# Which of several waits of one instruction is written first, in thirty places of a four-layer network kernel

## The chip, the cores and the metric

The kernel runs on one core of one Trainium2 chip. The metric is the device time of the core in microseconds (us), less being better. Several executions of one kernel are compared by their median.

## The reference, cut to what matters

The network takes x, 8 sequences of 256 rows of 128 numbers, and adds eight blocks to it one after the other, each behind a layer normalisation:

```python
x = x + L0_attn(layernorm(x))   # q, k, v as spike counts, 16 heads, softmax
x = x + L0_ffn(layernorm(x))    # FP4-quantized gate * up, down
x = x + L1_attn(layernorm(x))   # four Mamba layers
x = x + L1_ffn(layernorm(x))    # ternary weights, 128 -> 512
x = x + L2_attn(layernorm(x))   # causal linear attention
x = x + L2_ffn(layernorm(x))    # 8 experts of 512, top 1
x = x + L3_attn(layernorm(x))   # long convolution as two scans, projection, norm
x = x + L3_ffn(layernorm(x))    # dense 512 plus product-key retrieval, top 8
```

The core of a Mamba layer, for each of 256 channels d and 16 states s, is a recurrence over the 256 rows t:

```python
dA = jnp.exp(dt_t[:, :, None] * A)
h = dA * h + dt_t[:, :, None] * B_t[:, None, :] * u_t[:, :, None]
y = jnp.einsum('bds,bs->bd', h, C_t)
```

## The kernel before

Everything stays in on-chip memory as X, two tiles of 128 rows for each of the 8 sequences ("chunk" c). The work is cut into stages, and stages are put on five lines: `u` (setup), `f` (front), `s` (scan), `a` and `b` (the stages outside the Mamba layers, of even and odd chunks for the most part). A stage has one generator for each engine: `pe` (TensorE, PE), `dve` (VectorE, DVE), `act` (ScalarE, ACT), `pool` (GpSimd, POOL) and `sp` (SyncE, which issues the DMAs). Each `yield` ends a turn. The order of turns on each engine is written out by hand in the strings `ORDER`, and `take_turns` plays them: so each engine has one fixed list of instructions, in which the five lines alternate, and an instruction that waits holds all that stand behind it.

Each line has a semaphore for each engine, and each operation adds one to it (`then_inc`, with the name of the operation recorded by `tick`). `e.wait_ge(semaphore, value)` puts a wait before the next instruction of that engine. `n.dve("b3")` is the value that DVE's semaphore has when the operation `b3` is done. Where several waits stand before an instruction, all must come true; the order in which they are written has no part in what is computed.

The scan job k (32 of them, 8 chunks by 4 layers) works in 8 groups g of 4 states. Its steps for a group are:

- SP spreads dt and dt*u of the front over the partitions (`R[q]`, L1001); `landed` is the wait for such a transfer. `spread` is the wait for the B and C rows that the front has sent.
- ACT makes dA = exp(dt*A) in four instructions (`a`, L1025), into one of NA = 3 buffers; it waits for the scan that used the buffer last and, for g < 4, for the transfer.
- DVE multiplies dt*u by B into `dtuB`, a tile in PSUM (`b`, L1041), both inputs coming from SBUF, and then runs the recurrence over it (the scan `s`, L1049), which reads dA from SBUF and dtuB from PSUM. There is one `dtuB`, so `b` waits for the scan before it and the scan waits for `b`.
- POOL multiplies the result in place by C, in two instructions (`c`, L1060), once the scan is done.
- PE sums over the states (`y`, L1080) and frees one of NG = 6 result buffers, for which the scan six groups later waits.

The front (job k) makes dt, u, B and C for the scan; its output projection of job k - 2 is L947. The other places are in the stages of lines `a` and `b`: L643, L646 (there the copies of L427), L659, L668, L684, L698 and L711 in the attention of layer 0, L788 in its feed-forward stage, L1325 (values of the linear attention), L1390 to L1475 in the experts' stage, L1497 to L1550 in the convolution, L1620 to L1758 in the last stage.

In the experts' stage expert x has its first matrix product in L1467 (`h`), its ReLU on ACT in L1434, its second product in L1475 (`y`, over k = 0 to 3; k = 0 and k = 3 wait for ACT), and DVE adds the chosen rows to X in L1411. In the attention of layer 0 PE makes the scores of head h into one bank (L711), ACT takes the exponential (L668, `e`), and the next head's scores wait for that where there is one bank. The masks `m0` to `m3` for them are made by DVE in L627, once in the stage. `values` (L698) multiplies by v for four heads at a time.

Of the kernel before, what the change touches and what calls it, by code (L numbers as in the profile page):

```python
# [16 lines left out]
NL = 4  # L17
# [241 lines left out]
def program(nc, ap):  # L259
    with ExitStack() as ctx:  # L260
# [330 lines left out]
        class L0Attn(Stage):  # L591
# [43 lines left out]
            def pool(self, e, n, c):  # L635
# [4 lines left out]
                yield  # L640
                e.wait_ge(loaded["l0a"], 16)
                e.wait_ge(T.act, n.act("xn1"))
                e.tensor_tensor(X2(c), X2(c), row(w("l0a", "ob")), ALU.add).then_inc(T.pool, n.tick("ob"))  # L643
                yield
                e.wait_ge(U.pool, U.at(0, "pool", T.name))
                e.wait_ge(T.dve, n.dve("u3"))  # L646
# [3 lines left out]
            def act(self, e, n, c):  # L650
# [4 lines left out]
                yield  # L655
                e.wait_ge(loaded["l0a"], 16)
                e.wait_ge(T.pe, n.pe("qk"))
# [5 lines left out]
                for h in range(16):  # L663
                    if h >= 4:
                        e.wait_ge(T.pe, n.pe(f"z{h // 4 - 1}{h % 4}"))
                    e.wait_ge(T.pe, n.pe(f"s{h}"))
                    table(e, "exp")
                    e.activation(v.Pr[h % 4], score[h % len(score)], ACT.Exp, scale=SC).then_inc(T.act, n.tick(f"e{h}"))  # L668
                    yield
                yield from divide_act(e, n, T, T.banks[1], v, "z33")  # L670

            def pe(self, e, n, c):
# [7 lines left out]
                yield  # L680
                e.wait_ge(loaded["l0a"], 16)
                e.wait_ge(T.act, n.act("xT"))
# [10 lines left out]
                def values(j):  # L693
                    e.wait_ge(T.pool, n.pool("vz3"))
                    e.wait_ge(T.act, n.act(f"e{4 * j + 3}"))
# [8 lines left out]
                for h in range(16):  # L704
                    j, g = divmod(h, 4)
                    if h >= len(score):
                        e.wait_ge(T.act, n.act(f"e{h - len(score)}"))
                    if g == 0:
                        e.wait_ge(T.dve, n.dve(f"m{j}"))
# [18 lines left out]
        class L0Ffn(Stage):  # L728
# [48 lines left out]
            def pe(self, e, n, c):  # L777
# [4 lines left out]
                yield  # L782
                e.wait_ge(U.act, U.at(0, "act", "w3"))
                e.wait_ge(T.act, n.act("xT"))
# [45 lines left out]
        class Front(Stage):  # L830
# [106 lines left out]
            def pe(self, e, n, k):  # L937
                v, b = chains[k % 2], F.bank
                if k:
                    e.wait_ge(F.act, n.act(""))  # L940
                    e.wait_ge(F.dve, n.dve(""))
                if k >= 2:
                    c, l = UNITS[k - 2]
                    e.wait_ge(F.dve, n.dve("y"))
# [43 lines left out]
        class Scan(Stage):  # L988
# [22 lines left out]
            def act(self, e, n, k):  # L1011
# [4 lines left out]
                for g in range(8):  # L1016
                    at, q, h = 8 * k + g, g % 4, g // 4
                    if at >= NA:
                        job, was = divmod(at - NA, 8)
                        e.wait_ge(S.dve, S.at(job, "dve", f"s{was}"))  # L1020
                    if h == 0:
                        e.wait_ge(*self.landed(n, q, 0))
# [6 lines left out]
            def dve(self, e, n, k):  # L1029
                e.wait_ge(*self.spread(k, "B"))  # L1030
                if k == 0:
                    e.wait_ge(U.pool, U.at(0, "pool", f"wc{NL - 1}"))
                    for T in Os:
                        e.wait_ge(T.act, T.at(0, "act", "e15"))
                for g in range(8):
                    at, q, h = 8 * k + g, g % 4, g // 4
                    if at:
                        e.wait_ge(S.dve, n.dve(f"s{g - 1}") if g else S.at(k - 1, "dve", "s7"))
                    if h == 0:
# [3 lines left out]
                    yield  # L1043
                    if at >= NG:
                        job, was = divmod(at - NG, 8)
                        e.wait_ge(S.pe, S.at(job, "pe", f"y{was}"))
                    e.wait_ge(S.act, n.act(f"a{g}"))
                    e.wait_ge(S.dve, n.dve(f"b{g}"))
# [148 lines left out]
        class L2Attn(Stage):  # L1197
# [74 lines left out]
            def pe(self, e, n, c):  # L1272
# [45 lines left out]
                def values(j):  # L1318
                    e.wait_ge(T.pool, n.pool("vz3"))
                    e.wait_ge(T.act, n.act(f"p{2 * j + 1}"))  # L1320
# [31 lines left out]
        class L2Ffn(Stage):  # L1352
# [30 lines left out]
            def dve(self, e, n, c):  # L1383
                v, T = self, self.T
                enter_dve(e, n, T, c, True)
                yield from norm_dve(e, n, T, v, X2(c))
                e.wait_ge(loaded["mo"], 16)
                e.wait_ge(loaded["const"], 16)
                e.wait_ge(T.pe, n.pe("lg"))
# [12 lines left out]
                yield  # L1402
                e.wait_ge(T.act, n.act("xn1"))
                e.wait_ge(T.pe, n.pe("b2"))
# [530 lines left out]
```

## Time and profile before

| | us |
|---|---|
| three runs | 1868.27, 1875.47, 1875.95 (median 1875.47) |
| profiled execution | 1864.92 (span 1863.1) |
| PE busy, of the span | 1486.8 (80%) |
| DVE busy | 1501.9 (81%) |
| ACT busy | 1337.4 (72%) |
| POOL busy | 1241.6 (67%) |
| scans (L1049), 256 | 584.4 |
| `b` (L1041), 256 | 360.6 |
| `c` on POOL (L1060), 512 | 825.0 |

The profile is of one execution, which took less than the three runs. Its span is the time from the first to the last instruction. "Idle before" in a row is the time for which the engine did nothing just before the instructions of that row, and the names behind it say what ended that time. A chain of waits follows the last instruction back to what released it, step by step; a name with a q behind the engine (DVEq) is a step of that engine's sequencer, which waits or branches while the engine itself stays idle, and "issue" is time in which nothing that the profile shows was waited for. The chain of this profile goes back to 1243 us.

### The profile page before, as it was taken

What the parts mean: (1) busy time and instruction counts of PE and PEld (TensorE: products, weight loads), DVE (VectorE), ACT (ScalarE), POOL (GpSimd) and SP (SyncE); (2) the same over time, 40 slices, a digit from 0 to 9 for tenths busy, and PEclk for the clock granted to TensorE, in tenths of its full rate; (3) what the DMA queues carried; (4) which work ended last, traced back from release to release, by engine and by line L of the source; (5) the groups of instructions that cost most, each with busy time, mean ns of one, the idle gap of its engine ahead of it and who ended that gap; (6) DMA issues with size and microseconds to landing.
All of it is one profiled execution on the core that took longest, in us unless ns stands there. A gap on an engine that the chain in (4) does not pass through costs nothing. (4 is left out here: it accounts for less than half of the span.)

```text
span 1863.1 us, 27727 instructions
## 1 busy us (share of the span) xinstructions
PE 1486.8 (80%) x9417; PEld 1054.3 (57%) x9417; DVE 1501.9 (81%) x2326; ACT 1337.4 (72%) x2729; POOL 1241.6 (67%) x1255
## 2 busy tenths in 40 slices
PE   5767767657899987677878998778989986789975
PEld 2443434335576665544456777556667765667854
DVE  6588899899999899868898888888889998831254
ACT  4476756666898787776678878778888886654564
POOL 4158568777787778776666666777878887830046
PEclk9667677778999999677799999888999997889998
DMA  5033313423443542221235435241445432212300
GB/s 193 1 77 87 95 41 80 103 69 97 120 131 103 150 114 74 71 69 31 71 115 135 126 115 143 52 122 47 120 133 137 137 103 64 72 35 82 114 18 6
DMA packets 84588, 170.12 MB, mean 91 GB/s; under 512 B 9441, under 2 KB 14945, under 8 KB 84065
## 3 DMA queue, kind: packets, MB, share of 16 engines
q1 hardware_dynamic: 84448, 168.37, 33.1%
q8 instruction: 75, 1.23, 0.3%
q14 instruction: 65, 0.52, 0.1%
HBM read 99.12 MB, written 2.10 MB: 54 GB/s over the span
## 5 line engine op out<-in xcount | busy, mean ns | idle before, releaser
L1060 POOL TENSOR_TENSOR m<-m 128x512 f32<-128x512 f32 x512 | 825.0, 1633 | 131.0 <-DVE m L1049 125.6
L1049 DVE TENSOR_TENSOR_SCAN m<-m,dtuB 128x1024 f32<-128x1024 f32 x256 | 584.4, 2283 | 23.6 <-ACT m L1025 6.3
L1025 ACT ACTIVATE m<-m,Aneg 128x255 f32<-128x255 f32 x1024 | 428.5, 497 | 22.7 <-DMA m<-m 16.9
L1041 DVE TENSOR_TENSOR dtuB<-m 128x1024 f32<-128x1024 f32 x256 | 360.6, 1409 | 10.7 <-DMA m<-m 3.3
L1467 PE MATMUL ps<-o 128*128 128x256 f32 x512 | 149.2, 399 | 21.1 <-DVE X L1411 11.3
L1080 PE MATMUL ps<-m,w_const 128*32 128x256 f32 x2048 | 153.1, 425 | 9.6 <-POOL m L1060 9.5
L1434 ACT ACTIVATE o<-ps,w_mo 128x256 f32<-128x256 f32 x256 | 114.3, 471 | 62.1 <-PE ps L1467 60.9
L364 POOL TENSOR_TENSOR o<-o,mhalf 128x2 f32<-128x2 f32 x64 | 15.9, 249 | 202.5 <-DVE o L358 202.5
L964 PE MATMUL ps<-m,wc 128*128 128x256 f32 x512 | 138.6, 431 | 6.4 <-ACT m L385 6.4
L1475 PE MATMUL ps<-o 128*128 128x128 f32 x1024 | 129.5, 280 | 8.2 <-ACT o L1434 8.2
L1182 PE MATMUL ps<-o 128*128 128x256 f32 x512 | 123.8, 388 | 14.9 <-ACT o L1151 7.8
L1758 PE MATMUL ps<-w_const,o 128*128 128x128 f32 x512 | 89.8, 340 | 56.8 <-DVE o L1626 30.2
L1475 PEld LDWEIGHTS ps<-o 128*128 128x128 f32 x1024 | 122.5, 194 | 18.8 <-issue 13.7
L964 PEld LDWEIGHTS ps<-m,wc 128*128 128x128 f32 x512 | 110.2, 220 | 30.3 <-ACT m L385 9.3
L1758 PEld LDWEIGHTS ps<-w_const,o 128*128 128x128 f32 x512 | 82.5, 247 | 67.5 <-ACT o L1698 37.6
L668 ACT ACTIVATE o<-ps 128x512 f32<-128x512 f32 x112 | 66.2, 594 | 75.5 <-PE ps L711 48.9
L711 PE MATMUL ps<-o 32*128 32x256 bf16 x224 | 56.2, 343 | 78.9 <-ACT o L668 58.6
L1467 PEld LDWEIGHTS ps<-o 128*128 128x128 f32 x512 | 84.0, 189 | 55.1 <-ACT o L1434 22.1
L1182 PEld LDWEIGHTS ps<-o 128*128 128x128 f32 x512 | 94.2, 192 | 35.3 <-issue 15.6
L1080 PEld LDWEIGHTS ps<-m,w_const 128*32 128x32 f32 x2048 | 69.4, 120 | 77.9 <-issue 30.4
L347 ACT ACT_TABLE_LOAD x83 | 106.5, 1283 | 9.5 <-DMA w_mb<-in_mb 5.4
L1660 POOL TENSOR_TENSOR o<-o 128x512 f32<-128x512 f32 x64 | 85.9, 1343 | 15.2 <-DVE o L1620 13.6
(252 smaller groups left out, 2915.1 us busy)
## 6 DMA issues: line engine op xcount, KB each, us to landing
m<-m SPq DMA_DIRECT2D x256, 256.0 KB, 4.9
m<-spread SPq DMA_DIRECT2D x64, 512.0 KB, 4.9
o<-in_mox SPq DMA_DIRECT2D x128, 256.0 KB, 3.0
o<-in_l1x SPq DMA_DIRECT2D x88, 256.0 KB, 3.0
w_mb<-in_mb SPq DMA_DIRECT2D x1, 2288.0 KB, 12.2
m<-in_cwr SPq DMA_DIRECT2D x1, 2048.0 KB, 15.9
w_l3f<-in_l3f SPq DMA_DIRECT2D x1, 1536.0 KB, 17.4
X<-in_x SPq DMA_DIRECT2D x4, 256.0 KB, 7.1
```

Of the source, the lines that this page charges most:

```text
L347: e.preload_act_table_set("natural_log_exp_and_others")
L964: op = e.matmul(b[:, h * CH:h * CH + CH], wc[:, l, j, h * 128:h * 128 + 128], v.xT[:, j:j + CH], start=j == 0, stop=j == 3)
L1025: op = e.activation(dA[at % NA][:, j, 1:CH], R[q][:, h * CH + 1:h * CH + CH], ACT.Exp, scale=Aneg[:, l, 4 * g + j:4 * g + j + 1])
L1041: e.tensor_tensor(dtuB[:, :, :], bc(R[q][:, (2 + h) * CH:(3 + h) * CH].unsqueeze(1), 4, CH), Br[k % 2], ALU.mult).then_inc(S.dve, n.tick(f ...
L1049: e.tensor_tensor_scan(flat(G[at % NG]), flat(dA[at % NA]), flat(dtuB[:, :, :]), 0.0, ALU.mult, ALU.add).then_inc(S.dve, n.tick(f"s{g}"))
L1060: op = e.tensor_tensor(part, part, Cr[k % 2][:, j:j + 2, :], ALU.mult)
L1080: op = e.matmul(S.y[32 * q:32 * q + 32, h * CH:h * CH + CH], red, G[(8 * k + g) % NG][:, j, :], start=False, stop=j == 3, skip_group_check ...
L1182: op = e.matmul(b[:, 0:CH], v.ring[(at + j) % RING][:, cut(k)], src[:, k, :], start=k == 0, stop=k == 3)
L1434: e.activation(v.hd[x % 2][:, k, :], self.bank(5 * x + 4 + k)[:, 0:CH], ACT.Relu, bias=w("mo", "b1")[:, x, k:k + 1]).then_inc(T.act, n.tic ...
L1467: e.matmul(self.bank(5 * x + 4 + k)[:, 0:CH], v.ring[2 * x % RING][:, cut(k)], v.xT, start=True, stop=True).then_inc(T.pe, n.tick(f"h{x}{k}"))
L1475: op = e.matmul(self.bank(5 * x + 8)[:, cut(i)], v.hd[x % 2][:, k, cut(i)], v.ring[(2 * x + 1) % RING][:, cut(k)], start=k == 0 and i == 0 ...
L1758: op = e.matmul(a[:, cut(k)], v.Em[h % 2][:, cut(k)], ident, start=h == 0 and k == 0, stop=h == 3, skip_group_check=True)
```

## The change

In thirty places the order of the waits before one instruction is altered. Where a wait stood above a loop, it is now inside it under a condition, so that it still stands before the same instruction. No operation is added, taken away or moved on its engine, and no semaphore or value is another. The core of the diff:

```diff
@@ L0Attn, act (L668)
                 for h in range(16):
+                    e.wait_ge(T.pe, n.pe(f"s{h}"))
                     if h >= 4:
                         e.wait_ge(T.pe, n.pe(f"z{h // 4 - 1}{h % 4}"))
-                    e.wait_ge(T.pe, n.pe(f"s{h}"))
@@ L0Attn, pe (L711)
+                    if g == 0:
+                        e.wait_ge(T.dve, n.dve(f"m{j}"))
                     if h >= len(score):
                         e.wait_ge(T.act, n.act(f"e{h - len(score)}"))
-                    if g == 0:
-                        e.wait_ge(T.dve, n.dve(f"m{j}"))
@@ Front, pe (L947)
+                if k >= 2:
+                    e.wait_ge(F.dve, n.dve("y"))
                 if k:
                     e.wait_ge(F.act, n.act(""))
                     e.wait_ge(F.dve, n.dve(""))
                 if k >= 2:
                     c, l = UNITS[k - 2]
-                    e.wait_ge(F.dve, n.dve("y"))
@@ Scan, act (L1025)
+                    if h == 0:
+                        e.wait_ge(*self.landed(n, q, 0))
                     if at >= NA:
                         job, was = divmod(at - NA, 8)
                         e.wait_ge(S.dve, S.at(job, "dve", f"s{was}"))
-                    if h == 0:
-                        e.wait_ge(*self.landed(n, q, 0))
@@ Scan, dve (L1041 and L1049)
-                e.wait_ge(*self.spread(k, "B"))
-                if k == 0:
-                    e.wait_ge(U.pool, U.at(0, "pool", f"wc{NL - 1}"))
-                    for T in Os:
-                        e.wait_ge(T.act, T.at(0, "act", "e15"))
                 for g in range(8):
                     at, q, h = 8 * k + g, g % 4, g // 4
                     if at:
                         e.wait_ge(S.dve, n.dve(f"s{g - 1}") if g else S.at(k - 1, "dve", "s7"))
+                    if g == 0:
+                        e.wait_ge(*self.spread(k, "B"))
+                    if at == 0:
+                        e.wait_ge(U.pool, U.at(0, "pool", f"wc{NL - 1}"))
+                        for T in Os:
+                            e.wait_ge(T.act, T.at(0, "act", "e15"))
                     if h == 0:
                         e.wait_ge(*self.landed(n, q, 1))
                     e.tensor_tensor(dtuB[:, :, :], bc(R[q][:, (2 + h) * CH:(3 + h) * CH].unsqueeze(1), 4, CH), Br[k % 2], ALU.mult).then_inc(
                         S.dve, n.tick(f"b{g}"))
                     yield
+                    e.wait_ge(S.dve, n.dve(f"b{g}"))
+                    e.wait_ge(S.act, n.act(f"a{g}"))
                     if at >= NG:
                         job, was = divmod(at - NG, 8)
                         e.wait_ge(S.pe, S.at(job, "pe", f"y{was}"))
-                    e.wait_ge(S.act, n.act(f"a{g}"))
-                    e.wait_ge(S.dve, n.dve(f"b{g}"))
@@ Scan, pool (L1060)
-                e.wait_ge(*self.spread(k, "C"))
                 for g in range(8):
                     at = 8 * k + g
                     e.wait_ge(S.dve, n.dve(f"s{g}"))
+                    if g == 0:
+                        e.wait_ge(*self.spread(k, "C"))
@@ L2Ffn, dve (L1411)
                 for x in range(8):
+                    e.wait_ge(T.pe, n.pe(f"y{x}"))
                     e.wait_ge(T.dve, n.dve(f"x{x - 1}1" if x else "b2"))
-                    e.wait_ge(T.pe, n.pe(f"y{x}"))
@@ L2Ffn, act (L1434)
+                        e.wait_ge(T.pe, n.pe(f"h{x}{k}"))
                         if k == 0 and x >= 2:
                             e.wait_ge(T.pe, n.pe(f"y{x - 2}"))
-                        e.wait_ge(T.pe, n.pe(f"h{x}{k}"))
@@ L2Ffn, pe (L1475)
-                    e.wait_ge(*self.landed(n, 2 * x + 1))
                     for k in range(4):
                         if k in (0, 3):
                             e.wait_ge(T.act, n.act(f"h{x}{max(k, 2)}"))
+                        if k == 0:
+                            e.wait_ge(*self.landed(n, 2 * x + 1))
@@ L3Attn, dve (L1500)
+                e.wait_ge(T.dve, n.dve("xa"))
                 e.wait_ge(U.pool, U.at(0, "pool", "onesF"))
-                e.wait_ge(T.dve, n.dve("xa"))
@@ L3Ffn, dve (L1620)
-                    e.wait_ge(T.pe, n.pe(f"D{i}"))
                     for h in range(4):
-                        e.wait_ge(T.pool, n.pool(f"E{i}{h}"))
+                        if h % 2 == 0:
+                            e.wait_ge(T.pool, n.pool(f"E{i}{h}"))
                         if i or h:
                             e.wait_ge(T.pool, n.pool(f"w{i}{h - 1}" if h else f"w{i - 1}3"))
+                        if h % 2:
+                            e.wait_ge(T.pool, n.pool(f"E{i}{h}"))
+                        if h == 0:
+                            e.wait_ge(T.pe, n.pe(f"D{i}"))
@@ L3Ffn, pool (L1649)
+                            e.wait_ge(T.pool, n.pool(f"r{i}"))
                             e.wait_ge(T.dve, n.dve(f"fl{i}"))
-                            e.wait_ge(T.pool, n.pool(f"r{i}"))
```

The other places exchange two or three waits in the same way: at L643, L659, L684, L1390, L1497, L1524, L1550 and L1721 a value of another engine (`xn1`, `qk`, `xT`, `lg`, `gl`) now stands before the load of a weight pack; at L646 `u3` before a setup value; at L698 and L1325 ACT's `e` or `p` before POOL's `vz3`; at L788 `xT` before `w3`; at L1405 `b2` before `xn1`; at L1509 `o` before `pb`; at L1758 for h = 0 ACT's `w{i}0` before DVE's `x` or `d`.

## Rows read from the trace of the kernel before

**Rows 1.** Page, part 1: busy us, share of the span and instructions of each engine.

```profile
PE 1486.8 (80%) x9417; PEld 1054.3 (57%) x9417; DVE 1501.9 (81%) x2326; ACT 1337.4 (72%) x2729; POOL 1241.6 (67%) x1255
```

**Rows 2.** Busy time by stretch: us; PE, PEld, DVE, ACT, POOL; granted clock; DMA.

```profile
300.00:1640.00 1340.00, 1094.86 (x7100) 795.26 (x7098) 1181.14 (x1688) 1039.70 (x2130) 1007.24 (x961) 0.90 0.37 99
1650.00:1750.00 100.00, 97.39 (x652) 77.87 (x653) 18.62 (x76) 46.37 (x100) 6.17 (x24) 0.97 0.26 82
```

**Rows 3.** Chain of waits, 1420 to 1436 us: start us, us, what.

```profile
1425.92 0.03 issue
1425.95 0.05 DVEq L1048
1426.00 0.04 issue
1426.04 2.30 DVE m L1049
1428.34 0.03 DVEq L1040
...
1428.42 2.36 DVE dtuB L1041
...
1433.20 0.02 issue
1433.22 1.23 DVE dtuB L1041
```

**Rows 4.** DVE by line: count, busy us, mean ns, idle before and releasers.

```profile
L1049 DVE TENSOR_TENSOR_SCAN m<-m,dtuB 128x1024 f32<-128x1024 f32 x256 | 584.4, 2283 | 23.6 <-ACT m L1025 6.3 <-PE ps L1080 1.8
L1041 DVE TENSOR_TENSOR dtuB<-m 128x1024 f32<-128x1024 f32 x256 | 360.6, 1409 | 10.7 <-DMA m<-m 3.3
```

**Rows 5.** Timeline of DVE and POOL at 284 us: start us, us, what.

```profile
284.23 2.35 DVE L1041 TENSOR_TENSOR dtuB<-m 128x1024 f32<-128x1024 f32 x1
...
284.21 3.48 POOL L1060 TENSOR_TENSOR m<-m 128x512 f32<-128x512 f32 x2 [0.16 <-DVE m L1049]
```

**Rows 6.** Timeline of DVE and POOL around 425 us, a steady stretch.

```profile
425.39 1.23 DVE L1041 TENSOR_TENSOR dtuB<-m 128x1024 f32<-128x1024 f32 x1
...
429.08 1.23 DVE L1041 TENSOR_TENSOR dtuB<-m 128x1024 f32<-128x1024 f32 x1
...
421.76 3.53 POOL L1060 TENSOR_TENSOR m<-m 128x512 f32<-128x512 f32 x2 [0.16 <-DVE m L1049]
```

**Rows 7.** Chain of waits before L1475 (k = 3, then k = 0), L1060 and L1649.

```profile
1388.43 0.04 issue
1388.47 0.71 PE ps L1475 x4
...
1520.63 0.14 issue
1520.76 1.41 PE ps L1475 x5
...
1565.45 0.07 issue
...
1820.91 0.02 issue
1820.93 0.02 POOLq L1647
1820.95 0.09 issue
```

**Rows 8.** Who waited for whom: us in total, times, longest us.

```profile
PEld ps L711 <- ACT o L668: 92.0, 75, 4.3
```

**Rows 9.** Timeline of DVE and POOL at 764 us; chain at 1560 us.

```profile
763.34 4.82 POOL L1060 TENSOR_TENSOR m<-m 128x512 f32<-128x512 f32 x3
...
764.57 1.23 DVE L1041 TENSOR_TENSOR dtuB<-m 128x1024 f32<-128x1024 f32 x1
...
1560.64 2.39 DVE dtuB L1041
```

More of the change, by code:

```diff
@@ L640, in pool @@
                 yield
+                e.wait_ge(T.act, n.act("xn1"))
                 e.wait_ge(loaded["l0a"], 16)
-                e.wait_ge(T.act, n.act("xn1"))
                 e.tensor_tensor(X2(c), X2(c), row(w("l0a", "ob")), ALU.add).then_inc(T.pool, n.tick("ob"))
                 yield
+                e.wait_ge(T.dve, n.dve("u3"))
                 e.wait_ge(U.pool, U.at(0, "pool", T.name))
-                e.wait_ge(T.dve, n.dve("u3"))
                 spread_pool(e, n, T, v.va)
@@ L655, in act @@
                 yield
+                e.wait_ge(T.pe, n.pe("qk"))
                 e.wait_ge(loaded["l0a"], 16)
-                e.wait_ge(T.pe, n.pe("qk"))
                 for i, name in enumerate(("q", "k")):
@@ L680, in pe @@
                 yield
+                e.wait_ge(T.act, n.act("xT"))
                 e.wait_ge(loaded["l0a"], 16)
-                e.wait_ge(T.act, n.act("xT"))
                 for i, name in enumerate(("q", "k")):
@@ L693, in values @@
                 def values(j):
+                    e.wait_ge(T.act, n.act(f"e{4 * j + 3}"))
                     e.wait_ge(T.pool, n.pool("vz3"))
-                    e.wait_ge(T.act, n.act(f"e{4 * j + 3}"))
                     for kt in range(2):
@@ L782, in pe @@
                 yield
+                e.wait_ge(T.act, n.act("xT"))
                 e.wait_ge(U.act, U.at(0, "act", "w3"))
-                e.wait_ge(T.act, n.act("xT"))
                 for i in range(2):
@@ L1318, in values @@
                 def values(j):
+                    e.wait_ge(T.act, n.act(f"p{2 * j + 1}"))
                     e.wait_ge(T.pool, n.pool("vz3"))
-                    e.wait_ge(T.act, n.act(f"p{2 * j + 1}"))
                     for i in range(2):
@@ L1386, in dve @@
                 yield from norm_dve(e, n, T, v, X2(c))
+                e.wait_ge(T.pe, n.pe("lg"))
                 e.wait_ge(loaded["mo"], 16)
                 e.wait_ge(loaded["const"], 16)
-                e.wait_ge(T.pe, n.pe("lg"))
                 e.tensor_tensor(v.lg, self.bank(1)[:, 0:16].rearrange("p (a b) -> p a b", a=2), bc(w("mo", "gb").unsqueeze(1), 2, 8),
@@ L1402, in dve @@
                 yield
+                e.wait_ge(T.pe, n.pe("b2"))
                 e.wait_ge(T.act, n.act("xn1"))
-                e.wait_ge(T.pe, n.pe("b2"))
                 e.tensor_tensor(X2(c), ps2(self.bank(3)), X2(c), ALU.add).then_inc(T.dve, n.tick("b2"))
@@ L1493, in dve @@
                 yield from norm_dve(e, n, T, v, X2(c))
+                e.wait_ge(T.act, n.act("xT"))
                 e.wait_ge(loaded["l3a"], 16)
                 e.wait_ge(U.dve, U.at(0, "dve", "r7"))
-                e.wait_ge(T.act, n.act("xT"))
                 e.tensor_tensor(v.xa, v.xT, Apow[:, :], ALU.mult).then_inc(T.dve, n.tick("xa"))
+                e.wait_ge(T.dve, n.dve("xa"))
                 e.wait_ge(U.pool, U.at(0, "pool", "onesF"))
-                e.wait_ge(T.dve, n.dve("xa"))
                 e.tensor_tensor_scan(v.sc, bc(onesF[:, 0:1], CH), v.xa, 0.0, ALU.mult, ALU.add).then_inc(T.dve, n.tick("s0"))
@@ L1506, in dve @@
                 yield
+                e.wait_ge(T.pe, n.pe("o"))
                 e.wait_ge(T.pool, n.pool("pb"))
-                e.wait_ge(T.pe, n.pe("o"))
                 e.tensor_tensor(v.r, ps2(T.banks[1]), v.xn, ALU.add).then_inc(T.dve, n.tick("r"))
@@ L1521, in pool @@
                 yield
+                e.wait_ge(T.act, n.act("xT"))
                 e.wait_ge(loaded["l3a"], 16)
-                e.wait_ge(T.act, n.act("xT"))
                 e.tensor_tensor(v.xn, v.xn, row(w("l3a", "pb")), ALU.add).then_inc(T.pool, n.tick("pb"))
@@ L1546, in pe @@
                 yield
+                e.wait_ge(T.act, n.act("gl"))
                 e.wait_ge(loaded["l3a"], 16)
-                e.wait_ge(T.act, n.act("gl"))
                 for i in range(2):
@@ L1716, in pe @@
                 yield
+                e.wait_ge(T.act, n.act("xT"))
                 e.wait_ge(loaded["l3f"], 16)
-                e.wait_ge(T.act, n.act("xT"))
                 for k in range(2):
@@ L1751, in pe @@
                         yield
-                    e.wait_ge(T.dve, n.dve(f"x{i - 1}" if i else "d"))
                     for h in range(4):
                         e.wait_ge(T.act, n.act(f"w{i}{h}"))
+                        if h == 0:
+                            e.wait_ge(T.dve, n.dve(f"x{i - 1}" if i else "d"))
                         if h == 2:
```

## The prediction

> **What bounds the kernel now.** I read the page first: PE is busy 80% of the span, DVE 81%, ACT and POOL about 70% [rows 1]. No engine is full, so the stages matter. Between 300 and 1640 us, where the scans run, DVE is busy 1181 of 1340 us (88%); from 1650 to 1750 us PE is busy 97.39 of 100 us and DVE 18.62 [rows 2]. Each engine runs a fixed list in order, so a late instruction holds all behind it. The chain of waits for the scans then shows what one hand-over costs, and that is all this change can alter [rows 3].
>
> In it a scan (L1049) that comes straight after its `b` (L1041) begins 0.03 + 0.05 + 0.04 = 0.12 us after `b` ends, and the middle piece is DVEq L1048, a step of DVE's sequencer. The next `b` begins 0.02 us after that scan. The scan writes three waits (`y`, `a`, `b`), the `b` at 1433.22 one. PE shows the same: L1475 with two waits (k = 0) starts 0.14 us after ACT, with its single wait (k = 3) 0.04 us after [rows 7]. POOL's L1649 has such a step too (POOLq L1647). I conclude: the wait written first rides on the instruction, which is already queued when it comes true; the others sit in a separate step ahead, and if the last to come true is there, the engine still has to pass the step and fetch the instruction. The Trainium skill, "Perfetto Trace Analysis", Identifying Dependency Chains, says that extra waits may go into inserted EventSemaphore instructions; the trace agrees, with 0.05 us for DVEq L1048.
>
> **The change part by part.** No operation moves and no semaphore step disappears; only which wait rides changes.
>
> *Scan after `b` (L1046 to L1048).* In the timeline 118 of 256 scans follow their `b` directly (first at 118.86 us, last at 1613.40). The idle time before L1049 fits: 118 x 0.13 = 15.3, plus 6.3 for ACT and 1.8 for PE, is 23.4 of the 23.6 us shown [rows 4]. With `b` riding, each 0.12 should become 0.02: 118 x 0.10 = 11.8 us on DVE. In the other scans another DVE instruction stands between and hides the step: nothing. Where `a` is late (8 times) it stays in the step: nothing. Where `y` is last (3 idle times) 0.06 is lost each.
>
> *First `b` of a job (L1028 to L1041, g = 0).* Today `spread` rides and the previous scan stands in the step. The chain shows the result: the step at 1428.34, `b` at 1428.42, 0.08 after the scan, and it takes 2.36 us instead of 1.23 [rows 3]. Why: the multiply of POOL (L1060) waits for the same scan with its own riding wait and is a hair earlier; the first such pair starts at 284.21 (POOL) and 284.23 (`b`, 2.35 us) [rows 5]. A `b` that starts ahead of POOL takes 1.23. So 1.13 us is the price of losing that race. By the timeline 15 of the 32 first `b`s lose it so. After the change `b` starts 0.02 us after the scan and POOL 0.07 after it [rows 7], so `b` wins: 15 x (1.13 + 0.06) = 17.8 us on DVE. POOL's pair then lasts some 0.05 longer, as in the steady pairs, 3.53 against 3.48 [rows 5, 6]; nobody near the end waits for that. The Trainium skill, "SBUF — State Buffer", Who interferes with whom, says that a DVE instruction with two SBUF inputs contends with a GpSimd one that reads SBUF, and that issue order decides who blocks. That agrees with `b` (both inputs in SBUF) and with the scan, which reads one from PSUM and stays at 2.29.
>
> *All other places.* What a late wait costs in a step with one wait, against riding: POOL 0.02 + 0.02 + 0.09 = 0.13 before L1649 against 0.07 before L1060, so 0.06; PE 0.14 against 0.04, so 0.10 at most [rows 7]. For DVE I take 0.07, between POOL's 0.06 and the 0.10 of a step with two waits. No row shows ACT; from 0 to 0.10 are its ends, and I take 0.06 for it and for PE, since POOL's row is the one that shows the step itself. By the timeline the late wait sits in the step, with the engine idle for it, about 60 times on DVE (L1411 27, L1620 about 15 net, L1500 8, the rest L1390, L1405, L1509), 86 on ACT (L668 41, L1434 26, L1025 13, L659 6), 88 on PE (L1475 27, L947 17, the others 2 to 9 each) and 50 on POOL (L1060 21, L1649 16, L427 7, the rest 3 each). Sum: 4.2 + 5.2 + 5.3 + 3.0 = 17.7 us over four engines. Losses: at L711 the mask `m{j}` is made long before `e{h-1}` is there for h = 4, 8, 12, so this edit is the wrong way round. PE's weight loads wait there for ACT's L668 92.0 us in all [rows 8]; 13 of the 24 such waits come with an idle PE: 0.8 us. At L668 `z` is last 15 times: 0.9 us. Moving a DMA's wait (L1041, L1475, L1025) moves no DMA: SP's list is untouched, and a transfer that is late holds the same instruction as before.
>
> *What of it lies on the path.* The chain of waits covers the last 617 us. It holds 13 DVEq L1048 pieces, two of the five lost races of that stretch, and 22 other late waits in a step. 13 x 0.10 + 2 x 1.19 + 22 x 0.065 = 5.1 us in 617. Scaled by what the whole run has (118 against 23 direct hand-overs, 15 against 5 races, three times 22 others): 6.7 + 7.1 + 4.3 = 18 us. Paths beside it get shorter too, but not by as much everywhere, and cap the gain; I take 16 us. Bounds: if DVE were the path throughout, 11.8 + 17.8 + 4 = 34 us; if only the short gaps count and half of them, 6 us.
>
> **The rivals.** *POOL takes the port in the steady pairs (slower).* This is the place where the gain can turn. In the stretch at 425 us a scan and a `b` repeat every 3.69 us, and POOL needs 3.53 of them: its pair from 421.76 ends at 425.29, `b` starts at 425.39 [rows 6]. With 0.10 us less per period POOL ends as `b` starts. If `b` then found the port taken by POOL's next instruction it would take 2.36. Against it: a `b` at 764.57 started while POOL was in a run of three without a pause (763.34 to 768.16) and took 1.23 [rows 9], so starting in the tail of a POOL instruction can cost nothing; and POOL's next pair can't start before 0.07 after the scan, when `b` has begun. For it: the `b` at 1560.64 took 2.39 although POOL's instruction was about to end [rows 9]. It costs 1.13 a time; of 126 such pairs 16 lost eat the 18 us, and about a quarter (31, those whose POOL pair ends latest) would give 31 x 1.13 - 18 = 17 us more, times a path share of two thirds: about 1887 us.
>
> *The race is not won.* If `b` still comes second, the 7.1 us stay away: 11 us less a tenth, 1866 us.
>
> *Hidden elsewhere.* L1411 waits in DVE's list for PE, and from 1650 us PE is full [rows 2]; the freed time is waited away there: about 4 us, 1871 us.
>
> *It does nothing.* The lifecycle of a DVE instruction in the Trainium skill, "Perfetto Trace Analysis", Per-engine timelines, draws one wait queue in which all semaphores are satisfied; by that alone the order of writing would cost nothing. As a mechanism here: step and instruction pass at once whichever wait is last; 1875 us. The 0.12 against 0.02 in [rows 3] speak against it.
>
> **How the numbers follow.** The profiled execution took 1864.9 us (span 1863.1), below the three runs (1868.3 to 1876.0, median 1875.5); a change in stalls shifts both alike, so 1863.1 becomes 1847 and the median 1875.5 - 16 = 1859.5 us. Chances: forecast 0.70, race not won 0.12, hidden 0.08, nothing 0.04, slower 0.06. The range takes in the 34 us (1841) and reaches up to the case of nothing, 1875. About 0.5% (9.4 us) is what a measurement of this kernel can tell from no change. Faster by more than that: 0.70 and half of the second case, 0.76; within it: the other half, hidden and nothing, 0.18; slower 0.06.
>
> **What would show it.** In the profile after: idle before L1049 down from 23.6 to about 12 us; mean of L1041 down from 1409 to about 1340 ns, with `b` at 1.23 after a job's last scan; the step DVEq L1048 ahead of the end of `b`, so gone from the chain; L1649 and L1475 (k = 0) released in 0.07 and 0.04 us; L711 after L668 slower by 0.06 at h = 4, 8, 12. Wrong if L1041's mean rises (the port), or if these gaps shrink and the span doesn't.

## The result

| | before | after |
|---|---|---|
| runs, median (us) | 1875.47, 5 runs (1868.27 to 1876.88) | 1857.8, 5 runs (1854.7 to 1863.42) |
| ratio, with 95% interval | | 0.9922 (0.9894 to 0.9951) |
| profiled execution (us) | 1864.92, clock 0.878 | 1863.42, clock 0.864 |

A second measurement, on another occasion, gave 1871.01 us before (18 runs) and 1857.36 after (9 runs), a ratio of 0.9937 (0.9912 to 0.9963). The change makes the kernel 0.6 to 0.8% faster, 12 to 15 us. The ratios are those of the record and not quotients of the medians, which are 0.9906 (17.7 us) and 0.9927; both lie inside the intervals. The forecast was 1859.5 us.

The two profiled executions differ by 1.5 us only: that of before was faster than all five of its runs, and that of after was the slowest of its five. So the totals of these two traces say little, and what follows is read from their parts.

The profile after, page, part 1 (busy us, share of the span, instructions), to be held against [rows 1]:

```profile
PE 1502.0 (81%) x9417; PEld 1067.4 (57%) x9417; DVE 1492.5 (80%) x2326; ACT 1336.9 (72%) x2729; POOL 1240.3 (67%) x1255
```

DVE has 9.4 us less work with the same 2326 instructions. PE has 15.2 us more with the same 9417. Its granted clock fits that: a mean of 0.878 before and 0.864 after, with the two levels 2.4 and 1.2 GHz, is by estimate (1 - 0.878)/0.5 x 1863.1 = 455 us at the lower level before and 506 us after. Most of this isn't the work of the change: nine runs of the changed kernel ran between 0.863 and 0.878 (mean 0.870), and the 18 runs of the kernel before beside them between 0.866 and 0.882 (mean 0.873). The two traces also differ already in the first 100 us, before the first scan. Busy time by stretch (PE, PEld, DVE, ACT, POOL; granted clock; DMA), before and then after:

```profile
0.00:100.00 100.00, 65.38 (x330) 33.74 (x331) 63.94 (x159) 51.40 (x99) 29.28 (x70) 0.79 0.28 101
```

```profile
0.00:100.00 100.00, 66.12 (x326) 33.84 (x327) 64.08 (x159) 50.95 (x98) 27.35 (x69) 0.71 0.27 98
300.00:1640.00 1340.00, 1106.78 (x7110) 807.55 (x7109) 1176.39 (x1691) 1040.06 (x2131) 1009.29 (x962) 0.89 0.37 99
1650.00:1750.00 100.00, 97.65 (x654) 78.45 (x654) 18.24 (x74) 45.59 (x97) 6.17 (x24) 0.97 0.25 80
```

The last two lines answer [rows 2]: the stages are bound as before, DVE 88% busy between 300 and 1640 us and PE 98% from 1650 to 1750 us.

DVE by line after (count, busy us, mean ns, idle before and releasers). The scan is now L1051 and `b` is L1043; this answers [rows 4]:

```profile
L1051 DVE TENSOR_TENSOR_SCAN m<-m,dtuB 128x1024 f32<-128x1024 f32 x256 | 584.5, 2283 | 16.5 <-ACT m L1026 5.4 <-issue 3.6 <-PE ps L1083 2.8
L1043 DVE TENSOR_TENSOR dtuB<-m 128x1024 f32<-128x1024 f32 x256 | 349.7, 1366 | 9.5 <-DMA m<-m 3.1
```

The steps themselves are as many as before: in both traces the sequencers pass 651 semaphore steps on DVE, 385 on ACT, 543 on PE and 89 on POOL. So nothing was gained by having fewer of them; what changed is which wait sits in them.

The idle time before the scan is down from 23.6 to 16.5 us, and `b` takes 1366 instead of 1409 ns, 10.9 us in all. The chain of waits after (start us, us, what) shows the hand-overs of [rows 3] in the new form:

```profile
1560.85 0.02 issue
1560.87 2.30 DVE m L1051
1563.17 0.02 issue
1563.19 1.23 DVE dtuB L1043
```

and in two other places, the second product of an expert with k = 0 (0.04 where [rows 7] had 0.14) and POOL's L1657 (0.07 where it had 0.02 + 0.02 + 0.09):

```profile
1518.57 0.04 issue
1518.61 3.78 PE ps L1479 x16
...
1820.93 0.07 issue
1821.00 0.63 POOL o L1657
```

### The profile page after: what moved, and what is told of

The parts are those of the page before. It is cut to its first block, busy times and chain, and to the rows that moved or that the text cites. A ratio compares the mean times of both kernels' runs of the same rounds, so it can differ in the third digit from the quotient of the medians.

```text
span 1861.6 us, 27727 instructions
## 1 busy us (share of the span) xinstructions
PE 1502.0 (81%) x9417; PEld 1067.4 (57%) x9417; DVE 1492.5 (80%) x2326; ACT 1336.9 (72%) x2729; POOL 1240.3 (67%) x1255
## 3 DMA queue, kind: packets, MB, share of 16 engines
q8 instruction: 75, 1.23, 0.3%
## 4 chain that ended last, share of the span: by engine, by line
PE 48%; ACT 19%; DVE 18%; POOL 8%; issue 5%; DMA 2%; SPq 0%; DVEq 0%; ACTq 0%; POOLq 0%
DVE m L1051 6%; PE ps L1083 5%; ACT m L1026 4%; PE ps L1470 4%; POOL m L1063 4%; PE ps L965 4%; PE ps L1317 4%; PE ps L1185 4%; PE ps L1479 3%; DVE dtuB L1043 3%; PE ps L1767 3%; PE ps L1328 2%; PE ps L698 2%; PE ps L711 2%; ACT o L668 2%
## 5 line engine op out<-in xcount | busy, mean ns | idle before, releaser
L1051 DVE TENSOR_TENSOR_SCAN m<-m,dtuB 128x1024 f32<-128x1024 f32 x256 | 584.5, 2283 | 16.5 <-ACT m L1026 5.4
L1026 ACT ACTIVATE m<-m,Aneg 128x255 f32<-128x255 f32 x1024 | 428.5, 497 | 19.6 <-DMA m<-m 14.4
L1043 DVE TENSOR_TENSOR dtuB<-m 128x1024 f32<-128x1024 f32 x256 | 349.7, 1366 | 9.5 <-DMA m<-m 3.1
L1479 PE MATMUL ps<-o 128*128 128x128 f32 x1024 | 130.4, 281 | 7.6 <-ACT o L1437 6.8
L1185 PE MATMUL ps<-o 128*128 128x256 f32 x512 | 125.2, 391 | 12.5 <-ACT o L1154 6.7
L1479 PEld LDWEIGHTS ps<-o 128*128 128x128 f32 x1024 | 124.3, 196 | 17.7 <-ACT o L1437 13.5
L1767 PE MATMUL ps<-w_const,o 128*128 128x128 f32 x512 | 91.4, 344 | 53.1 <-DVE o L1634 31.6
L668 ACT ACTIVATE o<-ps 128x512 f32<-128x512 f32 x112 | 66.2, 594 | 76.9 <-PE ps L711 48.4
L1767 PEld LDWEIGHTS ps<-w_const,o 128*128 128x128 f32 x512 | 84.6, 252 | 63.4 <-ACT o L1706 54.8
L711 PE MATMUL ps<-o 32*128 32x256 bf16 x224 | 57.0, 348 | 78.0 <-ACT o L668 59.0
L1185 PEld LDWEIGHTS ps<-o 128*128 128x128 f32 x512 | 94.9, 193 | 32.9 <-issue 15.3
```

The lines of the kernel that those rows point to most:

```text
L1026: op = e.activation(dA[at % NA][:, j, 1:CH], R[q][:, h * CH + 1:h * CH + CH], ACT.Exp, scale=Aneg[:, l, 4 * g + j:4 * g + j + 1])
L1043: e.tensor_tensor(dtuB[:, :, :], bc(R[q][:, (2 + h) * CH:(3 + h) * CH].unsqueeze(1), 4, CH), Br[k % 2], ALU.mult).then_inc(S.dve, n.tick(f ...
L1051: e.tensor_tensor_scan(flat(G[at % NG]), flat(dA[at % NA]), flat(dtuB[:, :, :]), 0.0, ALU.mult, ALU.add).then_inc(S.dve, n.tick(f"s{g}"))
L1185: op = e.matmul(b[:, 0:CH], v.ring[(at + j) % RING][:, cut(k)], src[:, k, :], start=k == 0, stop=k == 3)
L1479: op = e.matmul(self.bank(5 * x + 8)[:, cut(i)], v.hd[x % 2][:, k, cut(i)], v.ring[(2 * x + 1) % RING][:, cut(k)], start=k == 0 and i == 0 ...
L1767: op = e.matmul(a[:, cut(k)], v.Em[h % 2][:, cut(k)], ident, start=h == 0 and k == 0, stop=h == 3, skip_group_check=True)
```

## The experiments

All ratios are to runs of the kernel before on the same chip, measured beside the others: 1870.78 us (35 runs) for the three parts and the later POOL alone; 1871.01 (18 runs) for the whole change again, its wrong places and the four steps more; 1870.47 (27 runs) for the two steps more, the parts taken out and the later POOL on top of the change. Their intervals are about 0.2% (4 us) to each side, so that single parts of this change can only just be told from nothing.

### The change in three parts

Before, with the waits of the scan alone written as in the change:

```diff
+                    e.wait_ge(S.dve, n.dve(f"b{g}"))
+                    e.wait_ge(S.act, n.act(f"a{g}"))
                     if at >= NG:
                         job, was = divmod(at - NG, 8)
                         e.wait_ge(S.pe, S.at(job, "pe", f"y{was}"))
-                    e.wait_ge(S.act, n.act(f"a{g}"))
-                    e.wait_ge(S.dve, n.dve(f"b{g}"))
```

> The kernel before with one edit alone: before the scan (L1049) the wait for `b` is written first. My theory: the 118 scans that follow their `b` directly start 0.035 us after it instead of 0.13; idle time before L1049 falls by about 11 us, b's durations stay as they are (mean 1409 ns, some 15 first `b`s of a job at 2.35 us), and the time falls by the path share of 11.4 us, 5 to 7 us (ratio 0.997). Rival (POOL takes the port in the steady pairs): L1041's mean rises and the time does not fall. Rival (order of writing does nothing): idle before L1049 stays 23.6 us and the time stays.

Before, with the first `b` of a job alone:

```diff
-                e.wait_ge(*self.spread(k, "B"))
...
                 for g in range(8):
...
+                    if g == 0:
+                        e.wait_ge(*self.spread(k, "B"))
```

> The kernel before with one edit alone: before the first `b` of a job the wait for the previous scan is written first, `spread` and the transfer after it. My theory (a race for the port): the 15 first `b`s that took 2.35 us take 1.23, the mean of L1041 falls from 1409 to about 1345 ns, idle before L1049 stays at 23.6 us; the time falls by 5 to 7 us (ratio 0.997). Rival (only the short gap counts): `b` still takes 2.35 us and the time falls by less than 1 us.

The change without these two places:

> The changed kernel with the two edits of DVE's part of the scan (L1041 and L1049 of before) undone; all other places stay changed. My theory: the first `b`s still lose the race, idle before the scan stays at 23 to 24 us, the late waits of POOL, PE and ACT are released 0.06 us earlier; the time falls by about 4 us (ratio 0.998), so most of the gain is not here. Rival (the gain is spread over all places by their number): 28 of 30 places are here, so most of the 14 us would be.

| kernel | median (us) | ratio (95%) | scan behind `b`, gap (ns) | idle before the scan (us) | mean of `b` (ns) | first `b`s over 2 us |
|---|---|---|---|---|---|---|
| before | 1870.78 | | 132 | 23.6 | 1409 | 16 |
| scan alone | 1863.41 | 0.9960 (0.9938 to 0.9982) | 35 | 14.4 | 1415 | 15 |
| first `b` alone | 1862.39 | 0.9952 (0.9933 to 0.9970) | 133 | 26.9 | 1341 | 2 |
| the rest alone | 1867.01 | 0.9984 (0.9961 to 1.0008) | 132 | 25.5 | 1405 | 16 |
| whole change | 1857.8 | 0.9922 (0.9894 to 0.9951) | 35 | 16.5 | 1366 | 4 |

(The gap is the median over the 125 scans whose `b` is the DVE instruction just before them; the whole change was measured on another occasion, beside runs of the kernel before at 1875.47 us.) Each part moves its own quantity; the idle time moves by some 3 us by itself. With the scan alone the times of `b` stay as they were:

```profile
L1049 DVE TENSOR_TENSOR_SCAN m<-m,dtuB 128x1024 f32<-128x1024 f32 x256 | 584.5, 2283 | 14.4 <-ACT m L1025 4.8 <-PE ps L1080 4.3 <-issue 0.7
L1041 DVE TENSOR_TENSOR dtuB<-m 128x1024 f32<-128x1024 f32 x256 | 362.2, 1415 | 12.9 <-DMA m<-m 5.8
```

In us, at 1871: 7.5 for the scan, 9.0 for the first `b`, 3.0 for the rest. The last one's interval includes no change at all, so that part is not shown.

### The race for the port, without touching DVE

Before, with one satisfied wait more, and so a step, ahead of POOL's product behind the eighth scan. It makes POOL later there and takes nothing away:

```diff
                     at = 8 * k + g
+                    if g == 7:
+                        e.wait_ge(U.pool, U.at(0, "pool", "onesF"))
                     e.wait_ge(S.dve, n.dve(f"s{g}"))
```

> The kernel before, and nothing is made earlier: POOL's multiply of the last group of each job (g = 7) gets a second wait, long true, which is written first, so that its wait for the scan stands in a step and POOL starts about 0.065 us later. My theory of the race: POOL at 0.13 us after the scan now comes behind the first `b` of the next job at 0.08, so the slow first `b`s fall from 15 to nearly 0 and the kernel gets faster by 5 to 7 us although one instruction is only delayed. Rival (the gain at the first `b` is that of its wait alone): nothing gets faster, the time is the same or up to 1 us more.

It came out at 1863.86 us, 0.9969 (0.9946 to 0.9992): delaying an engine made the kernel faster. Three first `b`s took over 2 us, `b` went from 1409 to 1349 ns on average, while the idle time before the scan did not fall:

```profile
L1049 DVE TENSOR_TENSOR_SCAN m<-m,dtuB 128x1024 f32<-128x1024 f32 x256 | 584.6, 2284 | 27.4 <-ACT m L1025 10.8 <-PE ps L1082 1.2
L1041 DVE TENSOR_TENSOR dtuB<-m 128x1024 f32<-128x1024 f32 x256 | 345.3, 1349 | 11.4 <-DMA m<-m 4.4
```

In these jobs `b` still starts 91 ns after the scan, as before, but POOL now starts 53 ns behind it instead of 12 ns ahead. The same edit on top of the change, where `b` is first anyway:

> The changed kernel, with one satisfied step more ahead of POOL's product behind the eighth scan, the edit that alone made the kernel before 0.31% faster. Theory (that edit helped only since it let DVE's first b take the port first, which the changed kernel does anyway): no gain, within 0.15% of the changed kernel, ratio to the kernel before 0.992 to 0.995, first b's over 2 us stay at 4 or fewer. Rival (a later POOL helps in another way, by what it does to the rest of DVE's or PE's work): 0.2% or more faster again, a ratio under 0.991.

1858.93 us, 0.9944 (0.9922 to 0.9967), three first `b`s over 2 us: no gain over the change's 0.9922 and 0.9937, and the rival's ratio under 0.991 lies outside the interval. As far as 0.2% can be told, a later POOL helps by the race and not otherwise.

### The whole change again, and its wrong places

The same kernel as the change, measured once more:

> The changed kernel as it is, to stand beside the two that follow on the same chip. Ratio to before 0.992 as first measured (0.9894 to 0.9951).

1857.36 us, 0.9937 (0.9912 to 0.9963); gap 35 ns, two first `b`s over 2 us, 19.3 us idle before the scan. So that idle time, 16.5 and 19.3 us in two executions of one kernel, is itself uncertain by some 3 us; over all seven traces here in which the scan's waits stand in the new order it is 13.4 to 19.3 us.

The change with L711 and L668 (h = 4, 8, 12) written the other way:

```diff
+                    if h >= 4 and h % 4 == 0:
+                        e.wait_ge(T.pe, n.pe(f"z{h // 4 - 1}{h % 4}"))
                     e.wait_ge(T.pe, n.pe(f"s{h}"))
-                    if h >= 4:
+                    if h >= 4 and h % 4:
                         e.wait_ge(T.pe, n.pe(f"z{h // 4 - 1}{h % 4}"))
...
-                    if g == 0:
-                        e.wait_ge(T.dve, n.dve(f"m{j}"))
                     if h >= len(score):
                         e.wait_ge(T.act, n.act(f"e{h - len(score)}"))
+                    if g == 0:
+                        e.wait_ge(T.dve, n.dve(f"m{j}"))
```

> The changed kernel with its two wrong-way places mended: at L711 ACT's `e` is written first again, at L668 `z` for h = 4, 8, 12 and `s` else. My theory: 12 idle waits of PE (0.104 to 0.042 us) and 15 of ACT (0.083 to 0.024) shrink, 1.6 us in sum, of which about a third to a half lies on the path: 0.5 to 1 us less than the changed kernel, too little for the clock to tell; the waits in the trace tell it. Rival (the attention of layer 0 sets the pace of the first 400 us): the full 1.6 us.

1859.63 us, 0.9926 (0.9898 to 0.9953). With the same done in four more places where the trace showed the late wait in the step (L1122, L1147, L1185, L1767):

> As the one before, and four further places: PE's L1767 (h = 2) writes `a5` first, DVE's first product and ACT's SiLU of the layer-1 feed-forward write the partner first, PE's second products there write ACT's wait before that for the transfer. My theory: some 10 waits of PE, 8 of ACT, 5 of PE and 3 of DVE shrink by 0.06: 1.6 us in sum, below 1 us on the path; in all 1 to 2 us faster than the changed kernel (ratio to before about 0.991). Rival: no difference or slower, since a transfer is last in some of them.

1856.79 us, 0.9920 (0.9894 to 0.9947). Both are the same as the change within the interval; a term of 2 us can't be measured here. No version that beats the change by a measurable amount came out of this.

### More steps

Before, with eight satisfied waits more at each scan, four ahead of `b` and `a` in the text and four behind. They make four steps more, and all four come to stand behind the step that waits for `b`:

```diff
+                    for _ in range(2):
+                        e.wait_ge(U.pool, U.at(0, "pool", "onesF"))
+                        e.wait_ge(U.act, U.at(0, "act", "A"))
                     e.wait_ge(S.dve, n.dve(f"b{g}"))
                     e.wait_ge(S.act, n.act(f"a{g}"))
+                    for _ in range(2):
+                        e.wait_ge(U.pool, U.at(0, "pool", "onesF"))
+                        e.wait_ge(U.act, U.at(0, "act", "A"))
```

> The kernel before with four more sequencer steps between the one that holds `b` and the scan: eight waits, all long true, are added before each scan. My theory: each costs 0.05 us, so a scan right behind its `b` starts about 0.33 us after it instead of 0.13, 24 us more idle time on DVE, of which the path share of 0.45 to 0.57 shows: 11 to 14 us slower (ratio 1.006 to 1.008). The slope gives that share without the port, since the first `b`s are not touched. Rival (DVE sets the pace throughout): the full 24 us, 1.013. Rival (such steps are passed ahead and cost nothing): idle before the scan stays at 24 us and the time stays.

It took 1913.31 us, 1.0224 (1.0196 to 1.0251): 42 us more, above what either theory had put down. The chain of waits shows why:

```profile
1447.43 1.24 DVE dtuB L1041
1448.68 0.04 DVEq L1051
1448.71 0.05 issue
1448.76 0.05 DVEq L1053
1448.81 0.05 issue
1448.86 0.05 DVEq L1054
1448.91 0.05 issue
1448.96 0.05 DVEq L1053
1449.01 0.05 issue
1449.05 0.05 DVEq L1054
1449.10 0.04 issue
1449.15 2.30 DVE m L1055
```

A step is not only its own 0.05 us; with the issue behind it each costs 0.1 here, and the median gap of the 125 direct scans is 480 instead of 132 ns, 87 ns for each step on average. And the cover that I had counted on elsewhere is too short for them: the scans that have another DVE instruction between `b` and them, which lost nothing before, account for 18 of the added 61 us:

```profile
L1055 DVE TENSOR_TENSOR_SCAN m<-m,dtuB 128x1024 f32<-128x1024 f32 x256 | 585.0, 2285 | 84.7 <-DVE dtuB L1041 40.3 <-issue 22.1 <-ACT m L1025 17.4
```

Half of it, with one such pair of waits on each side:

> The kernel before, with two more satisfied steps behind b ahead of each of the 256 scans (half of what the kernel with four more steps carries). With four, the 125 scans directly behind b start 480 ns after it instead of 132, that is 87 ns for each step, DVE's idle time before the scan rises from 23.6 to 84.7 us, and the kernel becomes 42 us longer, 0.69 us for each us of that idle time. Theory (each step costs the same, and some 0.7 of DVE's added idle time before the scan reaches the end): a gap of 306 ns, 50 to 54 us idle before the scan, 1889 to 1894 us where the kernel before takes 1871, a ratio of 1.010 to 1.012. Rival (the first steps vanish in slack and only many are paid): a ratio under 1.006.

1884.83 us, 1.0089 (1.0067 to 1.0111), a gap of 285 ns where 306 were expected. So the first two steps added 76 ns each, and the next two, from 285 to 480 ns, 98 each:

```profile
L1053 DVE TENSOR_TENSOR_SCAN m<-m,dtuB 128x1024 f32<-128x1024 f32 x256 | 584.5, 2283 | 50.1 <-DVE dtuB L1041 27.4 <-ACT m L1025 10.4 <-issue 4.6
```

The idle time is as expected, the time a little below the 1889 to 1894 us put down. This gives the share of DVE's waiting before a scan that reaches the end: 14.4 of 26.6 us, or 0.54, for two steps (16.6 us and 0.63 by the ratio 1.0089); 42.3 of 61.1, or 0.69, for four; and with the step made harmless 7.4 of 9.2, or 0.8, where the interval of 4 us on the time also allows 0.4. It is neither nothing nor everything, and no threshold is seen from which it sets in.

### Each part taken out of the whole

The change with the first `b`'s waits as before, and the change with the scan's waits as before:

> The changed kernel with the waits of the 32 first b's written as before; all else as changed. The race for the port is lost again: 15 or 16 first b's over 2 us, mean of b 1405 to 1415 ns instead of 1366, gap from b to scan 35 ns. Alone this part brought 0.48%, the scan's order 0.40% and the rest 0.16%, together 1.04%, where the whole change brings 0.78 and 0.63% in its two measurements. Theory (the parts lie partly on the same waiting time, so each is worth less beside the others): 0.20 to 0.35% slower than the whole change, a ratio to the kernel before of 0.9955 to 0.9965. Rival (the parts simply add up and the rest is scatter): 0.45% or more slower than the whole change, a ratio of 0.998 or above.

> The changed kernel with the waits of the scan written as before; all else as changed. Gap from b to scan 132 ns, 24 to 27 us idle before the scan, mean of b 1345 to 1370, at most 4 first b's over 2 us. Theory (the parts share their gain): 0.15 to 0.35% slower than the whole change, a ratio to the kernel before of 0.995 to 0.9965. Rival (they add up): 0.40% or more slower, a ratio of 0.997 or above.

The first took 1860.42 us, 0.9944 (0.9925 to 0.9963), with 15 first `b`s over 2 us, mean 1416 ns, gap 35 ns. The second took 1863.14 us, 0.9973 (0.9953 to 0.9992), with three over 2 us, mean 1352 ns, gap 132 ns. Against 0.993 for the whole, the mean of its two ratios, the first `b` is worth 0.14% there and the scan's order 0.43%. Alone they were worth 0.48 and 0.40%. By quotients of the medians it is 0.29 and 0.44%. For the scan's order that is the rival's side. For the first `b` it is below what even the theory of shared gain had put down (0.20 to 0.35%) by the one reckoning and inside it by the other. Two intervals of 0.2% stand behind each difference, and I can't call either settled; that the first `b` still saves time beside the rest is not shown. What the runs do settle is that each of the two moves its own quantity, the gap or the time of `b`, in both surroundings.

## Why the prediction was right, point by point

**The riding wait.** It was: the first written rides, the others cost a step. Right; it explains the gaps, and with the race below the first `b`s. Scans behind `b` start 35 ns after it instead of 132, that is 97 ns less, where 100 were put down. Over the other places the time from the last semaphore to the start, with the wait in a single step and then riding, is:

| engine | in a step (ns) | riding (ns) | taken in the prediction (us saved) |
|---|---|---|---|
| DVE | 92 | 24 | 0.07 |
| ACT | 83 | 24 | 0.06 |
| POOL | 133 | 68 | 0.06 |
| PE | 105 | 42 | 0.06 |

These are medians of the waits for which the engine sat idle. The bounds 0 and 0.10 for ACT, of which no row spoke, held. Where the late wait shares DVE's step with another, it costs 120 to 123 ns. The rival "it does nothing" falls with it. One reading in the prediction was wrong and did no harm: the `b` at 1433.22 of [rows 3] has two waits and not one. The wait for its transfer stands in a step (1430.94 to 1430.96) that was passed while the scan ran, and the wait for the scan rides, so it shows the riding wait even better. The Trainium skill, "Perfetto Trace Analysis", Per-engine timelines, draws one wait queue in which all semaphores are satisfied; 35 against 132 ns shows that this holds only for the wait that rides.

**The idle time before the scan.** Forecast about 12 us, measured 16.5, 19.3 and (scan alone) 14.4. The removed term is right to 0.4 us: 118 x 0.097 = 11.4 us where 11.8 were forecast. What is left was undersized: the 118 hand-overs of the forecast keep 0.035 and not 0.02 us each, 4.1 instead of 2.4 us, and single waits of 0.2 to 3.1 us for ACT, an issue and PE make up 5.4, 3.6 and 2.8 us, where the forecast had counted the former 6.3 and 1.8 for ACT and PE.

**The first `b`.** The mechanism is right, the count of races too high. Before, 15 first `b`s started right behind the scan with POOL's product just ahead, 14 of them by 11 or 12 ns, and took 2.3 us. After, 12 of the 15 start 35 ns behind the scan, POOL follows 45 ns later, and they take 1.23. The timeline of the job of [rows 5], DVE and then POOL:

```profile
282.66 2.29 DVE L1051 TENSOR_TENSOR_SCAN m<-m,dtuB 128x1024 f32<-128x1024 f32 x1
284.98 1.23 DVE L1043 TENSOR_TENSOR dtuB<-m 128x1024 f32<-128x1024 f32 x1
286.25 2.29 DVE L1051 TENSOR_TENSOR_SCAN m<-m,dtuB 128x1024 f32<-128x1024 f32 x1
...
285.03 3.53 POOL L1063 TENSOR_TENSOR m<-m 128x512 f32<-128x512 f32 x2
```

POOL loses nothing by it, because one product of its pair is long either way: 1.27 and then 2.25 us when POOL leads (before), 2.30 and then 1.27 us when `b` leads (after).

Three are still lost, at 147.66, 978.91 and 1465.73 us:

```profile
976.54 2.29 DVE L1051 TENSOR_TENSOR_SCAN m<-m,dtuB 128x1024 f32<-128x1024 f32 x1
978.91 2.34 DVE L1043 TENSOR_TENSOR dtuB<-m 128x1024 f32<-128x1024 f32 x1
...
978.90 3.47 POOL L1063 TENSOR_TENSOR m<-m 128x512 f32<-128x512 f32 x2
```

There the wait for the spread dt*u, which stands in the step, came true only 121 to 123 ns before `b` started, about when the scan ended; passing the step then took longer than POOL took. The prediction says that moving a DMA's wait moves no DMA and holds the same instruction as before; in these three its place decides the race. In the trace of the repeated run none of the three is lost. The first `b`s' time above 1.23 us fell from 18.1 to 5.7 us, 12.4, where 15 x 1.13 = 17 was forecast. The time that the other `b`s lose to the port stayed (27.3 and 28.8 us). The mean of `b` came to 1366 and not to the forecast's 1409 - 66 = 1343 ns, 5.9 us in all: 4.6 of them are first `b`s, mostly the three lost races, and 1.4 the other `b`s. That the port is what is lost, and not something else that comes with the order, is shown by the kernel with the later POOL: 91 ns after the scan as before, and yet 1.23 us. The Trainium skill, "SBUF — State Buffer", Who interferes with whom, says that issue order decides who blocks; 12 ns of it decide over 1.1 us here.

The traces show more than a fixed price. A `b` that starts inside a product of L1060 with more than 0.15 us of it left lasts until 1.08 to 1.10 us after that product's end, in all 52 such cases of the trace before and all 42 of the trace after: before, with 0.31, 0.60, 0.82 and 1.13 us of the product left it took 1.40, 1.69, 1.91 and 2.22 us (at 1523.77, 1000.68, 1481.84 and 1147.52 us). So the 1.13 us is the price of meeting a product at its start.

**POOL in the steady pairs (the slower rival).** It did not occur. The period of scan and `b` shrank from 3.69 to 3.59 us, and POOL works through without a pause, but `b` stays at 1.23:

```profile
418.31 1.23 DVE L1043 TENSOR_TENSOR dtuB<-m 128x1024 f32<-128x1024 f32 x1
419.58 2.29 DVE L1051 TENSOR_TENSOR_SCAN m<-m,dtuB 128x1024 f32<-128x1024 f32 x1
421.90 1.23 DVE L1043 TENSOR_TENSOR dtuB<-m 128x1024 f32<-128x1024 f32 x1
...
414.77 13.08 POOL L1063 TENSOR_TENSOR m<-m 128x512 f32<-128x512 f32 x7 [0.28 <-DVE m L1051]
```

POOL's next product can't start before the scan is done, and by then `b` is ahead of it by 45 ns. The tail of POOL's former pair costs `b` nothing: with 1 to 18 ns of a product left ten `b`s of this trace took 1.22 to 1.23 us, and six with 106 to 139 ns left as well. The `b` at 1560.64 of [rows 9], which the rival rested on, had 58 ns of a product left, but POOL's next product began 17 ns behind it and took 1.27 us, while `b` took 2.38: the tail was not what cost it.

**The losses.** As forecast in place and size: at L711 ACT's wait is in the step, 104 against 43 ns, 12 times with an idle PE; at L668 `z` is last exactly at h = 4, 8 and 12, 83 against 23 ns, 15 times. Together 0.7 + 0.9 us of engine time. That they cost the kernel anything was not measurable.

**What reaches the end.** The forecast was 6.7 us for the scan, 7.1 for the race and 4.3 for the rest, 18 in all, with 16 taken. Measured alone: 7.5, 9.0 and 3.0 us, each to within 4 us. The whole: 14.6 and 11.8 us. The share of the scan's term was taken as 6.7/11.8 = 0.57; the runs with more steps give 0.54 (0.63 by the ratio) and 0.69. That the terms come out so near is in part luck, two errors that cancel. Less time went from DVE than forecast: 9.2 us of idle time before the scan for 11.8, and 15.3 us of the first `b`s' time for 17 (12.4 in the whole change). And a larger share of it reached the end, by the medians and ratios some 0.8 for the scan and 0.6 for the race alone, where 0.57 and 0.40 were taken; the later POOL, with much the same saved on `b`, gives 0.4, so this share is known only roughly. The sum of the parts, 19.5 us, is more than the whole; the discount from 18 to 16 was too small rather than too large, but the sum and the whole differ by less than the intervals of the three parts together.

**The other rivals.** "The race is not won" held for three of 15 jobs. Hidden elsewhere: in the two traces the scan that starts at 1076 us is 7.7 us ahead of its twin, the last scan 2.9 us and the end 1.5 us. That looks like gain given back, and whether it is stays open: between 1200 and 1500 us the granted clock was 0.92 after and 0.94 before, and 0.86 against 0.92 from 1750 us on, and the runs, which average over the clock, show 12 to 15 us at the end. How much of the lead is waited away in front of PE is not separated by any run here.

**What the profile was to show.** The step DVEq of the scan is gone from the chain where `b` comes last, L1479 and L1657 are released in 0.04 and 0.07 us, and `b` after a job's last scan is at 1.23 in 12 of 15 cases. "Wrong if the gaps shrink and the span doesn't" came close to being read wrongly: the gaps shrank and the two profiled spans differ by 1.5 us. Only the runs show the 12 to 15 us.

## What to carry to other kernels

Where an instruction waits for several things, write first the one that comes last while its engine sits idle: here it saved 60 to 70 ns on each engine, and about 0.1 us where two waits shared DVE's step; where the engine was still busy with something longer than the step, it saved nothing. Before counting gaps, look for starts of two engines that are within some 10 ns of each other and want the same port, because there a small gap decides which of them is held until the other's instruction ends (here over up to 1.1 us), and a delay of the right engine can be a gain. Judge a change of under 1% by its runs and by the quantities it was to move, not by the spans of two profiles.

## What had not been expected

- A first `b` that starts 11 or 12 ns behind POOL's product takes 2.34 us, one that starts 45 ns ahead of it 1.23, and POOL's pair takes the same to within 0.05 us. One wait added on POOL, 64 ns, made the kernel 0.31% faster.
- A satisfied step costs DVE more than the 50 ns that its own piece of the chain shows, and the steps add up: 132, 285 and 480 ns with one, three and five of them, 76 ns each for the second and third, 98 each for the fourth and fifth.
- The granted clock of one kernel varies by itself from execution to execution, here from 0.863 to 0.878 in nine runs of the same program, and with it PE's busy time; between the two profiled executions PE's busy time differs by 15.2 us, as much as the whole gain.
